# A decoder recurrence on Trainium2: the shifted table loaded in two halves, the mask products ahead of the filter product

## The reference

```python
def step(carry, tgt):
    s, c, alpha = carry
    f = lax.conv_general_dilated(alpha, conv_w, (1,), 'SAME', ...)
    e = jnp.einsum('a,bta->bt', va, jnp.tanh(enc_proj + (s @ Wa_s.T)[:, None, :]
                                             + jnp.einsum('bft,af->bta', f, Wa_f) + ba))
    e = jnp.where(mask, e, jnp.float32(-1e+30))
    alpha_new = jax.nn.softmax(e, axis=1)[:, None, :]
    g = jnp.einsum('bt,btd->bd', alpha_new[:, 0], hbatch)
    y = jnp.tanh(g @ L_gy_w.T + L_gy_b + s @ L_sy.T) @ L_yy_w.T + L_yy_b
    rec = tgt @ L_ys.T + s @ L_ss.T + g @ L_gs_w.T + L_gs_b
    ig, fg, cg, og = jnp.split(rec, 4, axis=1)
    c_next = _sig(fg) * c + _sig(ig) * jnp.tanh(cg)
    s_next = _sig(og) * jnp.tanh(c_next)
    return ((s_next, c_next, alpha_new), y)
```

## Time and profile before

| | |
|---|---|
| median of 3 runs | 3463.73 us (3460.91 to 3466.06) |
| profiled execution | 3461.36 us, span 3459.6 us |
| mean granted TensorE clock | 0.959 |
| busy share of the span: PE, PEld, DVE, ACT, POOL | 88%, 60%, 57%, 49%, 8% |
| recurrence | about 1760 to 3123 us of the span |

### The profile page before, as it was taken

One profiled execution on the slowest core, in us unless ns is written; L12 is line 12 of the kernel. 1 busy time (PEld: TensorE's weight loads), 2 busy tenths in 40 slices (PEclk: granted clock), 3 DMA queues, 4 the chain that ended last, 5 costly groups with the idle time before them and its releaser, 6 DMA issues. The chain is left out here.

```text
span 3459.6 us, 107419 instructions
## 1 busy us (share of the span) xinstructions
PE 3027.8 (88%) x42778; PEld 2061.6 (60%) x42778; DVE 1975.7 (57%) x5170; ACT 1693.2 (49%) x4976; POOL 288.2 (8%) x994
## 2 busy tenths in 40 slices
PE   7876985667999999988989999999999999996998
PEld 4434552336777777754557666766676666664444
DVE  3776776885555555552045555555555555553665
ACT  3433544553444444441146666666666666663443
POOL 1002000000000000001000000000000000001332
PEclk9998997888999999999999999999999999998999
DMA  3003002001000000002123333333333333332000
GB/s 116 8 6 63 10 5 88 0 0 52 1 0 0 0 0 0 0 1 70 34 64 90 93 89 89 90 92 89 89 89 94 89 89 90 91 90 70 31 31 37
DMA packets 287970, 176.34 MB, mean 51 GB/s; under 512 B 23574, under 2 KB 277094, under 8 KB 287900
## 3 DMA queue, kind: packets, MB, share of 16 engines
q1 hardware_dynamic: 284860, 171.16, 17.1%
q0 software_dynamic: 3040, 4.23, 0.6%
HBM read 164.36 MB, written 14.16 MB: 52 GB/s over the span
## 5 line engine op out<-in xcount | busy, mean ns | idle before, releaser
L1994 PE MATMUL ps<-dm_hg,st_at 128*32 128x128 f32 x16384 | 516.3, 275 | 0.3 <-DVE st_at L2155 0.3
L1994 PEld LDWEIGHTS ps<-dm_hg,st_at 128*32 128x32 f32 x16384 | 424.5, 110 | 31.6 <-DVE st_at L2155 0.5
L2059 ACT ACTIVATE st_th<-ps,st_sw 128x128 f32<-128x128 f32 x1024 | 291.9, 368 | 238.9 <-PE ps L1966 238.9
L2138 DVE TENSOR_TENSOR st_th<-ps,st_sw 128x512 f32<-128x512 f32 x256 | 177.0, 692 | 159.3 <-PE ps L1966 159.3
L1955 PE MATMUL ps<-st_hk,dm_cwt 112*32 112x128 f32 x4096 | 164.7, 278 | 87.1 <-DMA st_hk<-padded_alignments 83.8
L1382 PE MATMUL ps<-sa_xt,w_wq 128*128 128x128 f32 x2048 | 239.9, 279 | 0.8 <-ACT sa_xt L1485 0.8
L1382 PEld LDWEIGHTS ps<-sa_xt,w_wq 128*128 128x128 f32 x2048 | 234.0, 194 | 4.9 <-issue 1.4
L1440 PE MATMUL ps<-sa_wo,sa_ct 128*128 128x512 f32 x512 | 222.6, 593 | 0.0
L1503 ACT ACTIVATE sa_pr<-sa_pr,sa_nm 128x128 f32<-128x128 f32 x512 | 197.7, 390 | 7.0 <-DVE sa_nm L1590 7.0
L1966 PE MATMUL ps<-st_fs,dm_waf 32*128 32x128 f32 x4096 | 186.5, 296 | 14.0
L1955 PEld LDWEIGHTS ps<-st_hk,dm_cwt 112*32 112x32 f32 x4096 | 100.3, 109 | 152.1 <-ACT st_gt L2078 104.9
(11 more groups left out here) (397 smaller groups left out, 5814.6 us busy)
## 6 DMA issues: line engine op xcount, KB each, us to landing
st_hk<-padded_alignments SPq DMA_DIRECT2D x254, 448.0 KB, 3.6
X<-in_x_dram SPq DMA_DIRECT2D x16, 512.0 KB, 9.8
out_dram<-X SPq DMA_DIRECT2D x16, 512.0 KB, 2.6
w_wq<-in_Wq_perm_dram SPq DMA_DIRECT2D x1, 4096.0 KB
sa_wo<-in_Wo_perm_dram SPq DMA_DIRECT2D x1, 4096.0 KB, 14.0
gate_inputs<-dp_ro SPq DMA_DIRECT2D x16, 256.0 KB, 2.3
st_rin<-gate_inputs SPq DMA_DIRECT2D x128, 32.0 KB, 3.3
rf_wf<-in_weightT_dram SPq DMA_DIRECT2D x8, 512.0 KB, 4.1
```

The source lines that it names most:

```text
L1994: ins = pe.matmul(R[g][32 * q:32 * q + 32, :], at[g][:, b, :], hg[:, BG * g + b, q * P:(q + 1) * P], start=False, stop=(b == BG - 1), tile ...
L2059: ins = act.activation(th[g][:, b, :], sums(g, 0)[:, b // 2, (b % 2) * P:(b % 2 + 1) * P], ACT.Tanh, bias=sw[g][:, b:b + 1])
L2138: dve.tensor_tensor(th[g][:, 4:8, :].rearrange("p (k s) n -> p k s n", s=2), sums(g, 1).rearrange("p k (s n) -> p k s n", s=2), sw[g][:, 4 ...
```

## The change

`hankel(g, i)` now describes every other batch row, from row i on, and two transfers with a semaphore each fill the even and the odd batch rows of `hk`. `filter_rows` waits for the even ones ahead of i = 0 and for the odd ones ahead of i = 1. The mask products leave the middle of the context parts and no longer wait for `sw_ready`: the mask of a group's next step is issued right ahead of its filter product, and for step 0 ahead of the loop. As the mask's `start=True` now comes ahead of the state term in the same bank, the state term is issued with `start=False`.

```diff
@@ sync
-                def hankel(g):
-                    return bass.AP(pad_d, g * BG * AW, [[1, TAPSA], [AW, BG], [1, P]])
+                def hankel(g, i):
+                    return bass.AP(pad_d, (g * BG + i) * AW, [[1, TAPSA], [2 * AW, BG // 2], [1, P]])
...
                             sp.wait_ge(ex_out[o], 16 * m + 16)
-                            sp.dma_start(hk[o][:, :, :], hankel(o)).then_inc(hk_in[o], 16)
+                            sp.dma_start(hk[o][:, 0:BG:2, :], hankel(o, 0)).then_inc(hk_even[o], 16)
+                            sp.dma_start(hk[o][:, 1:BG:2, :], hankel(o, 1)).then_inc(hk_odd[o], 16)
@@ tensor
                         def state_term(g, n):
                             pe.wait_ge(st_ready[g], n + 1)
-                            pe.matmul(SW[g], was[:, :], states(g), start=True, stop=True).then_inc(sw_ps[g], 1)
+                            pe.matmul(SW[g], was[:, :], states(g), start=False, stop=True, skip_group_check=True).then_inc(sw_ps[g], 1)

                         def filter_rows(g, n):
-                            if not isinstance(n, int) or n > 0:
+                            later = not isinstance(n, int) or n > 0
+                            if later:
                                 pe.wait_ge(gates_done[g], n)
-                                pe.wait_ge(hk_in[g], 16 * n)
                             for i in range(2):
+                                if later:
+                                    pe.wait_ge((hk_even if i == 0 else hk_odd)[g], 16 * n)
                                 for j in range(4):
                                     ins = pe.matmul(F[g][32 * j:32 * j + 32, :], cwt[:, i, :], hk[g][:, 2 * j + i, :],
...
                         def mask(g, n):
-                            pe.wait_ge(sw_ready[g], n + 1)
                             for j in range(4):
...
                             gates_of_context(g, n, 0)
-                            if front:
-                                mask(o, m)
                             gates_of_context(g, n, 1)
...
                             if more:
+                                mask(g, n + 1)
                                 filter_rows(g, n + 1)
...
                         for g in range(G5):
                             filter_rows(g, 0)
+                        for g in range(G5):
+                            mask(g, 0)
                         state_term(0, 0)
                         spread_filters(0, 0)
-                        mask(0, 0)
```

More of the change, by code:

```diff
@@ L1847, in stage_decoder @@
                 (at_ps, at_ready, r_sum, rec_ready, t_ps, gates_done, cc_done, tc_done, st_ready, sw_ps, sw_ready, filled0, filled1,
-                 f_ps, f_kept, conv_ps, added, th_done, e_ps, e_max, exp_done, al_ready, ex_out, hk_in, rin_in, hist_a, hist_s) = (
+                 f_ps, f_kept, conv_ps, added, th_done, e_ps, e_max, exp_done, al_ready, ex_out, hk_even, hk_odd, rin_in, hist_a, hist_s) = (
                     psems(n) for n in "at_ps at_ready r_sum rec_ready t_ps gates_done cc_done tc_done st_ready sw_ps sw_ready filled0 filled1 "
-                    "f_ps f_kept conv_ps added th_done e_ps e_max exp_done al_ready ex_out hk_in rin_in hist_a hist_s".split())
+                    "f_ps f_kept conv_ps added th_done e_ps e_max exp_done al_ready ex_out hk_even hk_odd rin_in hist_a hist_s".split())
                 R = [ps[:, 4 + g, 0:P] for g in range(G5)]
```

## The result

The changed kernel takes 3452.89 us (median of 11, 3444.9 to 3459.05) where the kernel before, in the runs beside it, takes 3463.29 (median of 11, 3456.89 to 3467.69). The ratio is 0.9971, 95% interval 0.9963 to 0.998: faster by 10 us, 7 to 13. The prediction was 3441, 22 us faster. The way was right, the size was half.

What follows compares the result with a forecast made beforehand. The recurrence's loop through DRAM was taken to bind. 127 turns x (0.22 - 0.05) plus 1 us for the mask took 22.6 us off 3461.36, giving 3438.8, a median near 3441; own range 3427 to 3457, wider range 3426 to 3462.

Steps and rivals of the forecast that it cites:

- What binds: Decoder recurrence: the round trip through DRAM sets the 10.67 us step; the engines' order alone would need about 10.16.
- The wait put down to ACT's gates: TensorE's 103.0 us wait ahead of the filter product, listed under ACT's gates; the prediction said the load came last.
- The odd load's landing: Second table load: lands when 448 KB are through, 3.6 us after the first issue, plus a second transfer's cost.
- d: Cost of the second transfer at the odd load's landing: taken as 0.05 us, floor 0, at most 0.2.
- the bound that the prediction had set for being wrong: Prediction is wrong if the odd load lands more than 3.5 us after its own issue.
- The tail: Filter product behind the odd landing: eight rows instead of sixteen, 0.22 us less, ends 0.20 and 0.32.
- The sum: Whole kernel: 127 turns x (0.22 - 0.05) = 21.6 us, plus 1 for the mask, 22.6 us off.
- SP's queue: Second load's issue on SP adds 0.35 us per half, hidden with 3.0 us of cover; uncovered, 89 us.
- The mask: Mask products moved ahead of the filter product: free in the gap there, gaining 1 us, between 0 and 3.
- no-change rival: d near 0.2 eats the 0.22, or the mask's 0.1 ahead of the filter counts fully: 3461 us, chance 0.11.
- The second start in series: Rival, between the filter product's halves: odd load pays about 2.0 us again, 226 us added, 3690; chance 0.09 including partial restart.

Runs made afterwards that it cites:

- x6: Changed kernel without the odd load and its wait, so half the table is left out: 3391.21 us, ratio 0.9805 to the kernel before.
- x1: Changed kernel, but the filter product waits for both loads ahead of its first matmul: 3481.87 us, ratio 1.008 to the kernel before.
- x7: Changed kernel, but ACT's queue issues the odd load, ahead of the first tanh: 3469.98 us, ratio 1.0032 to the kernel before.
- x5: Changed kernel with an unread 8 KB transfer issued between the even and odd loads: 3503.01 us, ratio 1.0132 to the kernel before.
- x4: Changed kernel with loads of seven batch rows and one, only the last matmul waiting for the second: 3429.16 us, ratio 0.9919 to the kernel before.
- x8: Changed kernel with loads of batch rows 0 to 5, then 6 and 7 (same column strip): 3440.4 us, ratio 0.9946 to the kernel before.
- x9: Changed kernel with loads of batch rows 1 to 6, then 0 and 7 (different column strips): 3422.68 us, ratio 0.9906 to the kernel before.

## Why the prediction was right in its direction and wrong in its size

*What binds: right.* The loop through DRAM sets a step and the engines' order is half a microsecond under it. Taking half of the load away gained 67 us and stopped at 10.13 per step (forecast 10.16). The wait put down to ACT's gates was indeed the load for the most part. With the odd load gone the gates run as before, yet the stage's waits of the filter product for them fell from 103.0 us to 9.9 (x6). They are nearly gone with the load in two as well, by the changed kernel's list of waits:

```profile
PEld ps L1958 <- DMA st_hk<-padded_alignments: 99.5, 286, 1.7
...
PEld ps L1958 <- ACT st_gt L2080: 13.9, 44, 0.8
```

Those of PEld for the loads were 40.3 before; with those of PE it is 126 us for the loads now and 123 before, so what fell away is what had been put down to the gates.

*The odd load's landing: the step that failed.* The prediction said that "its data stand behind the even ones, so it lands when 448 KB are through, 3.6, plus whatever a second transfer costs", and took 0.05 for that cost, d. It measured 0.22 (x1) and 3.81 against 3.61 (landings); the median from the odd issue, 3.5, is also the bound that the prediction had set for being wrong. That no bytes arrive sooner at the end held; they arrive later. What was wrong is the picture of 448 KB in one stream at the pace of the whole table. The even load moves at some 190 GB/s, alone or not, where the whole table has 320 to 340, and the odd load's data add to it only from about 2.0 us after the first issue. The issue was counted as 0.35, from the 0.31 of a lone issue; the second of two takes 0.49, so it ends 0.84 after the first began.

The runs bear this out. With the same two halves, the last landing is 3.6 with both issued at once from two queues (x7), 3.81 with 0.35 between the issues and 4.16 with 0.90 and a small transfer between them (x5). With a first load of 336 or 392 KB it is 3.55 to 3.6 (x4, x8, x9), and that load has about 300 GB/s in the quarter from 1.5 us, where the halves have 190. Why the even load is the slow one stays open: x4, x8 and x9 made the first load larger and its batch rows adjacent at once, and a load of rows 0 to 3 was not run. Against the rows' distance stands that rows 6 and 7 (x8) and rows 0 and 7 (x9) both land 3.2 after their issue and hold SP for 0.53. The nearest row for d, L1920 with up to 0.2, was the right size, and the prediction talked itself out of it with L1904, whose two loads of 32 KB are too small to show the pace of a long stream.

*The tail: right, too small.* Taken 0.22, measured 0.30 (x1 against the change). From the product's first weight load to the kept filters it was 0.73 us, from the second group's it is 0.50; and that weight load starts 0.04 after the landing instead of 0.10 (medians). The first is the forecast 0.22 to within 0.01, the second makes up the rest, and why it is so isn't shown.

*The sum.* 127 x (0.30 - 0.22) = 10 us; since the 0.30 was worked out from the measured 10, this is no check of its own. One is in the traces: from the issue of the table to the kept filters it is 4.46 us before and 4.37 after (means of 236 halves), and 127 x 0.09 = 11. Two errors of 0.17 and 0.08 per turn with opposite signs; the term d is the one that halved the gain.

*SP's queue: right.* The second issue is hidden there; the padded write still follows the exponentials by the same 0.5 us.

*The mask: small, as said.* 4 us alone and 3 beside x9 against the 1 taken (upper end 3); not a cost ahead of the filter, as the no-change rival had it. How much of the 4 is the gates' earlier start isn't separated from the spread of the runs.

*Rivals.* The second start in series (d = 2.0) didn't happen; d = 0.22 is just the point from which that rival would have decided. With its own tail of 0.22 the prediction would have ended at no gain but the mask's; only the tail that it had too small kept the change on the fast side, and that was luck.

## What to carry to other kernels

Two halves of a transfer issued one behind the other need not stream at the pace of the whole. Here a split into 224 + 224 KB landed 0.20 us later than the 448 KB in one, a split into 336 + 112 or 392 + 56 KB as early, and a first load of 224 KB was slow even with nothing behind it. So make the first part the large one and put behind the second only work that can run side by side. Look where the wait goes: with seven and one it went to the first load. Take the price of a back-to-back issue from a row of a back-to-back issue, and before an issue is moved to an engine that seems idle, see when that engine's idle time ends.

## What the runs showed of the hardware that was not expected

The same kind of transfer held SP for 0.31 us when issued after a pause and 0.49 when issued right behind another (0.52 to 0.54 for a smaller second part in x4, x8 and x9). Issued from SP and ACT at the same instant, 2304.13, they took 0.31 and 0.37. A load of 224 KB landed in 2.9 us alone, 3.1 with another behind it, and one of 448 KB in 3.6: while they stream, the small one has about 190 GB/s (x6) and the large one 320 to 340, both in rows of 512 B. Two such small loads issued at once from two queues reach 340 together (x7, mean of the quarters from 2.0 us).
